# First cross-attention of an eight-layer kernel: output tiles copied by ScalarE and added to X by GpSimd, statistics one turn later

## The chip, the cores and the metric

One core of a Trainium2 chip. The metric is the device time of the whole program in microseconds (us).

## The reference, cut to what matters

The reference is a stack of four pairs of cross-attention and feed-forward network over `x` of shape (8, 256, 128), with a context of shape (8, 64, 128), all in fp32. Each member of a pair works on the normed stream and is added to it. The change touches the first attention and the statistics of the norm behind it:

```python
# first attention, on the layer-normed x; h = 16 heads of 8, one k head and one v head for all
q = x @ Wq
k, v = jnp.split(context @ Wkv, 2, axis=-1)
sim = jnp.einsum('bhnd,btd->bhnt', q * scale, k)
att = jax.nn.softmax(sim, axis=-1)
y = jnp.einsum('bhnt,btd->bhnd', att, v)
return y @ Wo            # added to the residual stream
# then the first feed-forward network (a soft mixture over 1024 slots) on the norm of that sum
```

## The kernel before, in words

The residual stream lives in SBUF as `X`, 16 tiles of 128 tokens by 128 features; batch b owns tiles 2b and 2b+1. The program is written per engine: each engine's order of work is written out by hand, and the engines are joined by semaphores. The first attention is a software pipeline over the 16 token tiles. Every engine has a loop over t (NT = 16), and one pass of it is called a turn here. In turn t:

- **TensorE**: `similarities(t)` (recorded as L1763) writes the 128x1024 scores of tile t into two PSUM banks; `weights_T(t-1)` transposes the exponentials of tile t-1 (eight transposes, L1820), once they are there; `values(t-2)` multiplies them with v and sums them (32 small matmuls, L1763); `outputs0(t-3)` multiplies tile t-3 with `wo0` into PSUM bank 7 (L1763). In turns 2, 6 and 10, called grouped turns, TensorE also transposes four tiles of the normed x and projects them to queries in the middle of the rest, and the transposes of the exponentials are split around that.
- **VectorE**: the maximum over the keys (L1343), the subtraction of the maximum (L1346), the reciprocal of the denominators of tile t-2 (L1354), the multiplication by it (L1355), and the addition of the output of tile t-3 to `X` out of PSUM (L1359), which signals `x_done`. In turn 5 it also takes the statistics of the slot embeddings (L1312 to L1318). After the fourth, eighth, twelfth and sixteenth addition, in turns 6, 10, 14 and 18, `norm_behind` takes the statistics of the four finished tiles for the next norm (L1229, L1232, L1236).
- **ScalarE**: in grouped turns the copies of the normed x and of the queries (L813, L843); then the copy of the transposed exponentials to SBUF (L813, 128x1024), then the exponential of tile t (L874, 128x1024).
- **GpSimd**: it builds the block-diagonal keys of batches 1 to 7 (`keys(b)`, L739), applies the norm to the slot embeddings (L753 to L755), and for each finished group of four tiles computes the power and applies the norm (`ln_power(1, g)`: L612, L619, L620).

`outputs0(u)` waits for `y_ready` (L1355 of tile u) and for `x_done` of tile u-1, since bank 7 holds one output. VectorE's maximum of turn t+1 stands in its queue behind everything of turn t. Behind the loop come the logits of the slots: `bmax(0)` (L1333) is VectorE's in turn 17; `bmax(1)`, `bmax(2)` and `brec(0)` follow its loop; GpSimd's L764 needs `brec(0)`, and TensorE's `dispatch_T(0)` (L1927) needs L764. ScalarE goes on with `bexp(0)` (L891).

Of the kernel before, what the change touches and what calls it, by code (L numbers as in the profile page):

```python
# [46 lines left out]
def build_program(nc, A, out):  # L47
    with ExitStack() as ctx:
# [111 lines left out]
        y0T = carve(2, P)  # L160
        mx0 = carve(2, H0)
        rden0 = carve(P)
        ctxTd = carve(B * 2 * C)
        slot_raw = carve(ES // P, D)
        slot_n = carve(ES // P, D)
# [167 lines left out]
        av_ready = sem("av_ready")  # L333
        y_ready = sem("y_ready")
        out_ready = sem("out_ready")
        bl_ready = sem("bl_ready")
        bmax_done = sem("bmax_done")
        bexp_done = sem("bexp_done")
# [236 lines left out]
        def _(pool):  # L575
# [151 lines left out]
            for L in range(LAYERS):  # L727
                if L == 7:
                    pool.wait_ge(x_done, NT * 6)
                    edges = xpad[:, :, :].rearrange("p h (b n) -> p h b n", b=B)  # L730
                    pool.memset(edges[:, :, :, 0:1].bitcast(F32), 0.0)
                    pool.memset(edges[:, :, :, N + 1:N + 2].bitcast(F32), 0.0)
                    pool.memset(share.bitcast(F32), 1.0 / 32.0).then_inc(pool_made, 1)
                    quantised_norm()
                    continue
                if L == 0:

                    def keys(b):
                        pool.tensor_tensor(kbd[:, b], wide(krep[:, b * C:(b + 1) * C].unsqueeze(1), H0 // 2, C),  # L739
                                           wide(rowmask[:, :].unsqueeze(2), H0 // 2, C), ALU.mult).then_inc(kbd_done[1], 1)  # L740

                    ln_power(0, 0)
                    ln_power(0, 1)
                    pool.wait_ge(krep_done, 1)
                    keys(1)
                    ln_power(0, 2)
                    keys(2)
                    keys(3)
                    ln_power(0, 3)
                    for b in range(4, B):  # L750
                        keys(b)
                    pool.wait_ge(se_var, 1)
                    then(pool.tensor_tensor(srstd[:, 1, :], srstd[:, 0, :], neghalf[:, 0:ES // P], ALU.pow))  # L753
                    then(pool.tensor_tensor(slot_n, slot_raw, wide(smv[:, :, 0:1], ES // P, D), ALU.subtract))
                    pool.tensor_tensor(slot_n, slot_n, wide(srstd[:, 1, :].unsqueeze(2), ES // P, D), ALU.mult).then_inc(se_n, 1)  # L755
                    continue
                for g in range(NG):
                    if L != 1 or g < NG - 1:
                        ln_power(L, g)
                if L == 1:  # L760

                    for k in range(4 * B):
                        pool.wait_ge(brec_done, k + 1)
                        pool.tensor_tensor(qb[:, k % 4], qb[:, k % 4], wide(recB[:, k % 4].unsqueeze(2), 2, N), ALU.mult)\  # L764
                            .then_inc(bnorm_done, 1)
                        if k == 3:
                            ln_power(1, NG - 1)
                    experts0_low()
                    pool.wait_ge(xh_lo, E0)
                    pool.memset(eo[:, :, :, D:D + 1], 1.0).then_inc(pool_made, 1)  # L770
                if L == 2:

                    pool.wait_ge(ln_xn, NG * L + NG)
                    pool.tensor_tensor(X[:, :, :], X[:, :, :], wide(rows[:, ROW["qv1_b"], :].unsqueeze(1), NT, D), ALU.add)\
                        .then_inc(xbias_done, 1)

                    then(pool.memset(sel1, 0.0))
                    per_expert = sel1.rearrange("p a (e i) -> p (a e) i", i=8)
                    then(pool.affine_select(out=per_expert, in_=per_expert, compare_op=ALU.not_equal, fill=1.0, base=0,
                                            pattern=[[-1, E1], [0, 8]], channel_multiplier=1))  # L780
                    pool.affine_select(out=per_expert, in_=per_expert, compare_op=ALU.not_equal, fill=1.0, base=-E1,
                                       pattern=[[-1, E1], [0, 8]], channel_multiplier=1).then_inc(pool_made, 1)
                if L == 3:
                    experts1_low()
                if L == 4:

                    pool.wait_ge(x_done, NT * L)
                    then(pool.memset(sel2, 0.0))
                    per_expert = sel2.rearrange("p g (e i) -> p (g e) i", i=P // 4)
                    for part in range(3):  # L790
                        last = pool.affine_select(out=per_expert, in_=per_expert, compare_op=ALU.not_equal, fill=1.0, base=-E2 * part,
                                                  pattern=[[-1, E2], [0, P // 4]], channel_multiplier=1)
                        if part < 2:
                            then(last)
                    last.then_inc(pool_made, 1)
                    pool.wait_ge(wgu_hi, STEPS0 + NC1 + 1)
                    pool.tensor_tensor(w2r[:, 1], w2all, w2r[:, 0].bitcast(F32), ALU.subtract).then_inc(wgu_lo, 1)
                if L == 5:
                    pool.wait_ge(x_done, NT * L)
                    experts2_low()  # L800
                if L == 6:
                    pool.wait_ge(ln_xn, NG * L + NG)
                    pool.tensor_tensor(X[:, :, :], X[:, :, :], wide(rows[:, ROW["o3_b"], :].unsqueeze(1), NT, D), ALU.add)\
                        .then_inc(xbias_done, 1)
                    for k in range(3):
                        pool.wait_ge(w3_hi, k + 1)
                        pool.tensor_tensor(hh[:, k, 1, :], w3f[:, k, :], hh[:, k, 0, :].bitcast(F32), ALU.subtract).then_inc(w3_lo, 1)
# [3 lines left out]
        def _(act):  # L811
# [39 lines left out]
            token_rows(0)  # L851
            queries(0)

            for t in range(NT + 3):
                g = (t + 2) // 4
                if t == 1:
                    act.wait_ge(kv_mm, 2)
                    act.wait_ge(consts, 2)
                    vps = psum[:, 6, 256:256 + B * HD].rearrange("p (b d) -> p b d", b=B)
                    for par in range(2):  # L860
                        for r in range(2):
                            at = 16 * par + HD * r
                            last = copy(vstrip[C * r:C * r + C, :, par, at:at + HD], vps[C * r:C * r + C])
                    last.then_inc(vstrip_done, 1)
                if t % 4 == 2 and t < NT - 2:
                    token_rows(g)
                    queries(g)
                if 1 <= t <= NT:
                    weight_rows(t - 1)
                if t < NT:  # L870
                    act.wait_ge(sim_used, t + 1)
                    if t >= 2:
                        act.wait_ge(et_ready, t - 1)
                    act.activation(simE[:, t % 2, :], simS[:, t % 2].rearrange("p h k -> p (h k)"), ACT.Exp).then_inc(exp_done, 1)  # L874
                if t == NT:

                    act.wait_ge(se_n, 2)
                    for g in range(2):
                        act.wait_ge(se_tp, g + 1)
                        act.activation(seT[:, 512 * g:512 * g + 512], bank(g), ACT.Identity, scale=slot_gs[:, 0:1], bias=slot_gs[:, 1:2])\  # L880
                            .then_inc(se_T, 1)
                    for g in range(2):
                        ln_evac_group(1, g)
# [329 lines left out]
        def _(dve):  # L1213
# [122 lines left out]
                        accum_out=nmB[:, k % 4, c:c + 1])  # L1336
                last.then_inc(bmax_done, 1)

            for t in range(NT + 3):
                if t < NT:  # L1340
                    dve.wait_ge(sim_ready, t + 1)
                    sim = psum[:, 2 * (t % 2):2 * (t % 2) + 2, :].rearrange("p a (h k) -> p (a h) k", k=C)
# [8 lines left out]
                if 2 <= t <= NT + 1:  # L1351
# [1 line left out]
                    dve.wait_ge(av_ready, u + 1)  # L1353
                    then(dve.reciprocal(rden0, psum[:, 6, P:2 * P]))  # L1354
                    dve.tensor_tensor(y0T[:, u % 2, :], psum[:, 6, 0:P], rden0, ALU.mult).then_inc(y_ready, 1)  # L1355
                if t >= 3:
                    u = t - 3
                    dve.wait_ge(out_ready, u + 1)
                    dve.tensor_tensor(X[:, u, :], X[:, u, :], psum[:, 7, 0:D], ALU.add).then_inc(x_done, 1)  # L1359
                    norm_behind(1, u)  # L1360
                if t == NT + 1:
                    bmax(0)

# [397 lines left out]
        def _(pe):  # L1761
# [75 lines left out]
            def outputs0(u):  # L1837
                if u == 0:
                    pe.wait_ge(w_slots, 16 * N_SLOTS)
                pe.wait_ge(y_ready, u + 1)  # L1840
                if u >= 1:
                    pe.wait_ge(x_done, u)
                mm(psum[:, 7, 0:D], y0T[:, u % 2, :], wo0[:, :]).then_inc(out_ready, 1)

            def logits_slots(k):
# [660 lines left out]
```

## Time and profile before

| | us |
|---|---|
| median of three runs (986.33 to 987.37) | 987.25 |
| the profiled execution, device time | 984.96 |
| its span | 983.2 |
| busy in the span: TensorE / VectorE / GpSimd / ScalarE | 913.7 / 719.9 / 572.7 / 521.5 |

The first attention takes the first tenth of the span: its first maximum starts at 12.66 us and its last addition at 90.65 us. The page's chain of waits reaches back only to 798 us, so this stage has to be read from its timeline. In a timeline row the bracket at the end gives the idle time of the engine just before it, and what ended it; gaps under 0.15 us are not shown. A row with xN stands for N instructions in one. Instructions of one engine overlap a little at their ends, so the distance between two starts can be shorter than the first one's duration.

### The profile page before, as it was taken

The page shows a single profiled execution, that of the slowest core. Times are in us where ns is not written, and L with a number is a line of the kernel's source. Part 1 is how long each engine was busy: PE and PEld are TensorE (multiplying, and loading weights), DVE is VectorE, ACT ScalarE, POOL GpSimd, SP SyncE. Part 2 cuts the span into 40 slices and gives each one's busy share as a digit, 9 for nine tenths or more (in the row PEclk, how much of TensorE's full clock was granted, in tenths as well). Part 3 has the DMA queues.
Part 4 walks back from the last instruction along what each step waited for, and adds up shares of the span by engine and source line. Part 5 has one row for each costly group of instructions (what it writes and reads, how often), then busy time and mean ns, then how long its engine had stood idle before and what let it go on. Part 6 is the DMA issues. An engine that isn't in the chain of part 4 may idle for free. (4 is left out here: it accounts for less than half of the span.)

```text
span 983.2 us, 16388 instructions
## 1 busy us (share of the span) xinstructions
PE 913.7 (93%) x4925; PEld 700.8 (71%) x4925; DVE 719.9 (73%) x1657; ACT 521.5 (53%) x991; POOL 572.7 (58%) x542
## 2 busy tenths in 40 slices
PE   7897998989896899999999999999999889999796
PEld 5555775666694856888888888888887766667564
DVE  6897776899464788766666666666667888886865
ACT  3455665544634256666666666666663334453354
POOL 5512544677513156777777777777776538884500
PEclk9999999999997989999999999999999689999998
DMA  6000000322000000000000000000002000000001
GB/s 193 1 2 2 1 1 11 88 71 66 12 1 27 2 9 14 25 25 24 24 24 24 24 24 24 24 24 24 25 3 108 1 0 1 1 1 1 1 11 33
DMA packets 27113, 24.01 MB, mean 24 GB/s; under 512 B 3420, under 2 KB 23988, under 8 KB 26804
## 3 DMA queue, kind: packets, MB, share of 16 engines
q1 hardware_dynamic: 27059, 23.34, 8.0%
q8 instruction: 29, 0.48, 0.2%
q14 instruction: 25, 0.20, 0.1%
HBM read 22.28 MB, written 1.05 MB: 24 GB/s over the span
## 5 line engine op out<-in xcount | busy, mean ns | idle before, releaser
L1763 PE MATMUL psum<-xw 128*128 128x512 f32 x1248 | 324.3, 396 | 3.9 <-DVE xw L1400 2.6
L664 POOL TENSOR_TENSOR hh<-arena,hh 128x512 fp32r<-128x512 f32 x176 | 228.2, 1296 | 81.7 <-ACT hh L813 80.0
L1763 PEld LDWEIGHTS psum<-xw 128*128 128x128 f32 x1248 | 233.4, 189 | 56.5 <-issue 7.2
L1599 DVE TENSOR_TENSOR psum<-psum,arena 128x512 f32<-128x512 f32 x176 | 123.1, 700 | 99.6 <-PE psum L1763 93.2
L813 ACT ACTIVATE hh<-arena 128x512 fp32r<-128x512 f32 x228 | 143.1, 629 | 47.7 <-DVE arena L1698 45.3
L1046 ACT ACTIVATE arena<-psum 128x512 f32<-128x512 f32 x176 | 105.3, 598 | 119.0 <-PE psum L1763 118.9
L1763 PE MATMUL psum<-hh,wdn 128*128 128x512 f32 x528 | 148.4, 390 | 0.2 <-POOL hh L664 0.2
L1604 DVE TENSOR_TENSOR arena<-psum,arena 128x512 f32<-128x512 f32 x176 | 121.7, 692 | 8.9 <-DVE psum L1599 2.9
L1763 PEld LDWEIGHTS psum<-hh,wdn 128*128 128x128 f32 x528 | 98.9, 188 | 21.1 <-POOL hh L664 0.5
L1763 PE MATMUL psum<-arena 128*32 128x128 f32 (+7 forms) x1032 | 94.0, 307 | 12.8 <-ACT arena L813 6.5
L612 POOL TENSOR_TENSOR rstd<-veps,neghalf 128x4 f32<-128x4 f32 x28 | 28.2, 1010 | 106.1 <-DVE veps L1238 76.0
L1763 PEld LDWEIGHTS psum<-arena 128*32 128x32 f32 (+4 forms) x1032 | 69.1, 148 | 25.0 <-issue 11.4
L813 ACT ACTIVATE arena<-psum 128x512 f32<-128x512 f32 (+7 forms) x84 | 57.1, 694 | 50.4 <-PE psum L1763 19.6
L701 POOL TENSOR_TENSOR hh<-arena,hh 128x512 fp32r<-128x512 f32 x48 | 62.1, 1295 | 33.3 <-ACT hh L813 31.8
L764 POOL TENSOR_TENSOR tail<-tail 128x512 f32<-128x512 f32 x32 | 33.3, 1041 | 43.4 <-DVE tail L1370 43.4
L1763 PE MATMUL psum<-hh,w2r 128*128 128x512 f32 x144 | 46.7, 417 | 2.0 <-POOL hh L701 1.0
L624 POOL TENSOR_TENSOR xw<-egu,xw 128x256 fp32r<-128x256 f32 x32 | 27.6, 864 | 31.8 <-ACT xw L813 31.5
L891 ACT ACTIVATE tail<-arena,tail 128x256 f32<-128x256 f32 x64 | 32.0, 500 | 26.1 <-DVE tail L1333 26.1
L928 ACT ACTIVATE tail<-psum,ebias 128x512 f32<-128x512 f32 x32 | 22.0, 688 | 44.5 <-PE psum L1763 36.9
L635 POOL TENSOR_TENSOR arena<-arena,xn (+1 forms) x32 | 42.8, 1343 | 1.2 <-ACT xn L813 1.2
L1690 DVE SCALAR_TENSOR_TENSOR arena<-psum,arena 128x512 f32<-128x512 f32 x48 | 33.1, 691 | 11.7 <-PE psum L1763 9.6
L1763 PE MATMUL psum<-xw,w2r 128*128 128x512 f32 x144 | 41.6, 401 | 0.0
(288 smaller groups left out, 1536.1 us busy)
## 6 DMA issues: line engine op xcount, KB each, us to landing
egu<-in_w SPq DMA_DIRECT2D x44, 128.0 KB, 2.0
egu<-in_egu SPq DMA_DIRECT2D x16, 256.0 KB, 2.6
edn<-in_w SPq DMA_DIRECT2D x44, 64.0 KB, 1.8
edn<-in_edn SPq DMA_DIRECT2D x16, 128.0 KB, 2.0
arena<-in_w SPq DMA_DIRECT2D x1, 1536.0 KB, 6.8
X<-in_x SPq DMA_DIRECT2D x4, 256.0 KB, 4.6
arena<-in_conv SPq DMA_DIRECT2D x1, 1024.0 KB, 8.8
out<-X SPq DMA_DIRECT2D x4, 256.0 KB, 2.3
```

The costliest lines, as they stand in the source:

```text
L612: pool.tensor_tensor(rstd[:, s], veps[:, s], neghalf[:, s], ALU.pow).then_inc(ln_rstd, 1)
L635: pool.tensor_tensor(part, part, wide(shift_row(b).unsqueeze(1), 2, N), ALU.subtract).then_inc(pt_shifted, 1)
L664: pool.tensor_tensor(hh[:, s % 4, 1, :], h1[:, s % 2, :], hh[:, s % 4, 0, :].bitcast(F32), ALU.subtract).then_inc(hh_lo, 1)
L701: pool.tensor_tensor(hh[:, n % 4, 1, :], h2[:, n % 2, :], hh[:, n % 4, 0, :].bitcast(F32), ALU.subtract).then_inc(hh_lo, 1)
L764: pool.tensor_tensor(qb[:, k % 4], qb[:, k % 4], wide(recB[:, k % 4].unsqueeze(2), 2, N), ALU.mult)\
L813: return act.activation(dst, src, ACT.Copy)
L891: last = act.activation(qb[:, k % 4, c, :], logit_part(k // 4, 2 * (k % 4) + c, 1).rearrange("p a n -> p (a n)"), ACT.Exp, scale=-1.0, bia ...
L1046: act.activation(sil[:, k, :], bank(k), ACT.Silu).then_inc(nl_done, 1)
L1599: dve.tensor_tensor(bank(2 + k), bank(2 + k), sil[:, k, :], ALU.mult).then_inc(prod_done, 1)
L1604: dve.tensor_tensor(h1[:, k, :], bank(2 + k), rwb[:, s // 4, own], ALU.mult).then_inc(hid_done, 1)
L1690: dve.scalar_tensor_tensor(v2w[:, n % 3, :], bank(q), 0.0, cB[:, 0 if n < 4 * NG else 1, 512 * q:512 * q + 512], ALU.max, ALU.mult)\
L1763: return pe.matmul(dst, lhsT=lhsT, rhs=rhs, start=start, stop=stop)
```

## The change

VectorE's addition in the loop is gone. ScalarE copies the output of tile t-4 from PSUM to one of two new SBUF buffers at the head of turn t, and GpSimd adds it to `X`. The loops of ScalarE and VectorE have one turn more. `outputs0(u)` waits for the copy and not for the addition. The statistics are taken in turns 7, 11, 15 and 19. GpSimd takes the additions between its other work, with `ln_power(1, 0)` to `ln_power(1, 2)` written out among them.

```diff
--- before.py
+++ after.py
@@ -160,6 +160,7 @@
         y0T = carve(2, P)
         mx0 = carve(2, H0)
         rden0 = carve(P)
+        o0 = carve(2, D)
         ctxTd = carve(B * 2 * C)
         slot_raw = carve(ES // P, D)
         slot_n = carve(ES // P, D)
@@ -333,6 +334,7 @@
         av_ready = sem("av_ready")
         y_ready = sem("y_ready")
         out_ready = sem("out_ready")
+        o0_sb = sem("o0_sb")
         bl_ready = sem("bl_ready")
         bmax_done = sem("bmax_done")
         bexp_done = sem("bexp_done")
@@ -747,15 +749,26 @@
                     keys(2)
                     keys(3)
                     ln_power(0, 3)
+
+                    def added(u):
+                        pool.wait_ge(o0_sb, u + 1)
+                        pool.tensor_tensor(X[:, u, :], X[:, u, :], o0[:, u % 2, :], ALU.add).then_inc(x_done, 1)
+
                     for b in range(4, B):
                         keys(b)
+                        added(b - 4)
                     pool.wait_ge(se_var, 1)
                     then(pool.tensor_tensor(srstd[:, 1, :], srstd[:, 0, :], neghalf[:, 0:ES // P], ALU.pow))
                     then(pool.tensor_tensor(slot_n, slot_raw, wide(smv[:, :, 0:1], ES // P, D), ALU.subtract))
                     pool.tensor_tensor(slot_n, slot_n, wide(srstd[:, 1, :].unsqueeze(2), ES // P, D), ALU.mult).then_inc(se_n, 1)
+                    added(4)
+                    for g in range(NG - 1):
+                        ln_power(1, g)
+                        for u in range(4 * g + 5, 4 * g + 9 if g < 2 else NT):
+                            added(u)
                     continue
                 for g in range(NG):
-                    if L != 1 or g < NG - 1:
+                    if L != 1:
                         ln_power(L, g)
                 if L == 1:
 
@@ -851,8 +864,14 @@
             token_rows(0)
             queries(0)
 
-            for t in range(NT + 3):
+            for t in range(NT + 4):
                 g = (t + 2) // 4
+                if t >= 4:
+                    u = t - 4
+                    act.wait_ge(out_ready, u + 1)
+                    if u >= 2:
+                        act.wait_ge(x_done, u - 1)
+                    copy(o0[:, u % 2, :], psum[:, 7, 0:D]).then_inc(o0_sb, 1)
                 if t == 1:
                     act.wait_ge(kv_mm, 2)
                     act.wait_ge(consts, 2)
@@ -1336,7 +1355,7 @@
                         accum_out=nmB[:, k % 4, c:c + 1])
                 last.then_inc(bmax_done, 1)
 
-            for t in range(NT + 3):
+            for t in range(NT + 4):
                 if t < NT:
                     dve.wait_ge(sim_ready, t + 1)
                     sim = psum[:, 2 * (t % 2):2 * (t % 2) + 2, :].rearrange("p a (h k) -> p (a h) k", k=C)
@@ -1353,11 +1372,8 @@
                     dve.wait_ge(av_ready, u + 1)
                     then(dve.reciprocal(rden0, psum[:, 6, P:2 * P]))
                     dve.tensor_tensor(y0T[:, u % 2, :], psum[:, 6, 0:P], rden0, ALU.mult).then_inc(y_ready, 1)
-                if t >= 3:
-                    u = t - 3
-                    dve.wait_ge(out_ready, u + 1)
-                    dve.tensor_tensor(X[:, u, :], X[:, u, :], psum[:, 7, 0:D], ALU.add).then_inc(x_done, 1)
-                    norm_behind(1, u)
+                if t >= 4:
+                    norm_behind(1, t - 4)
                 if t == NT + 1:
                     bmax(0)
 
@@ -1839,7 +1855,7 @@
                     pe.wait_ge(w_slots, 16 * N_SLOTS)
                 pe.wait_ge(y_ready, u + 1)
                 if u >= 1:
-                    pe.wait_ge(x_done, u)
+                    pe.wait_ge(o0_sb, u)
                 mm(psum[:, 7, 0:D], y0T[:, u % 2, :], wo0[:, :]).then_inc(out_ready, 1)
 
             def logits_slots(k):
```

## Rows read from the trace of the kernel before

**Rows 1.** Windows, turns 6 to 15: busy us of PE, PEld, DVE, ACT, POOL; PEclk.

```profile
43.00:86.00 43.00, 38.36 (x478) 25.16 (x477) 38.81 (x76) 22.93 (x25) 10.34 (x10) 0.98 0.01 2
```

**Rows 2.** Timeline of turns 7 and 8 (start us, duration us, instruction).

```profile
48.97 0.96 DVE L1354 RECIPROCAL arena<-psum 128x128 f32<-128x128 f32 x1 [0.64 <-PE psum L1763]
...
49.25 1.13 PE L1763 MATMUL psum<-arena 64*128 64x512 f32 x4
49.96 0.29 DVE L1355 TENSOR_TENSOR arena<-psum,arena 128x128 f32<-128x128 f32 x1
50.17 0.28 DVE L1359 TENSOR_TENSOR X<-X,psum 128x128 f32<-128x128 f32 x1
...
50.42 1.23 DVE L1343 TENSOR_REDUCE arena<-psum 128x16 f32<-128x1024 f32 x1
...
54.05 1.09 PE L1820 MATMUL psum<-ident,arena 128*128 128x128 f32 x8 [0.16 <-ACT arena L874]
```

**Rows 3.** Timeline of turns 11 and 12, TensorE and VectorE.

```profile
63.69 1.09 PE L1820 MATMUL psum<-ident,arena 128*128 128x128 f32 x8 [1.00 <-ACT arena L874]
...
65.86 0.96 DVE L1354 RECIPROCAL arena<-psum 128x128 f32<-128x128 f32 x1
...
67.32 1.23 DVE L1343 TENSOR_REDUCE arena<-psum 128x16 f32<-128x1024 f32 x1
```

**Rows 4.** Timeline of turns 14 and 15, VectorE, and GpSimd's norm of group 2.

```profile
74.88 1.22 DVE L1343 TENSOR_REDUCE arena<-psum 128x16 f32<-128x1024 f32 x1
...
78.78 0.87 DVE L1229 BATCH_NORM_STATS2 stats<-X 128x6 f32<-128x128 f32 x4
...
80.17 1.22 DVE L1343 TENSOR_REDUCE arena<-psum 128x16 f32<-128x1024 f32 x1
...
82.55 1.04 POOL L620 TENSOR_TENSOR xn<-xn,rstd 128x512 f32<-128x512 f32 x1
```

**Rows 5.** Groups by form (busy us, mean ns), nearest rows of the new operations.

```profile
L660 POOL TENSOR_TENSOR wdn<-edn,wdn 128x128 fp32r<-128x128 f32 x44 | 20.8, 473 | 0.0
...
L1124 ACT ACTIVATE arena<-psum 128x128 f32<-128x128 f32 x1 | 0.3, 278 | 2.2 <-PE psum L1763 2.2
```

**Rows 6.** Waits from 12 to 96 us: total us, times, longest us.

```profile
ACT arena L813 <- PE psum L1820: 18.6, 16, 1.5
```

**Rows 7.** Timeline of turn 10, TensorE's values and ScalarE's first copy.

```profile
58.15 1.08 PE L1763 MATMUL psum<-arena 128*32 128x128 f32 x32
58.26 0.60 ACT L813 ACTIVATE xnT<-psum 128x512 f32<-128x512 f32 x1 [0.48 <-PE psum L1800]
```

**Rows 8.** Timeline of GpSimd, the slot norm's first and last instruction.

```profile
38.47 1.64 POOL L753 TENSOR_TENSOR arena<-arena,neghalf 128x8 f32<-128x8 f32 x1 [7.82 <-DVE arena L1317]
...
42.17 1.90 POOL L755 TENSOR_TENSOR arena<-arena 128x1024 f32<-128x1024 f32 x1
```

**Rows 9.** Timeline of turn 6, TensorE's values.

```profile
39.85 1.08 PE L1763 MATMUL psum<-arena 128*32 128x128 f32 x32 [2.37 <-DVE arena L1355]
```

**Rows 10.** Timeline from turn 16 to the first dispatch transposes.

```profile
83.79 1.09 PE L1820 MATMUL psum<-ident,arena 128*128 128x128 f32 x8 [1.90 <-ACT arena L874]
...
89.52 0.29 DVE L1355 TENSOR_TENSOR arena<-psum,arena 128x128 f32<-128x128 f32 x1
...
90.15 0.46 PE L1763 MATMUL psum<-wo,arena 128*128 128x128 f32 x2 [0.40 <-DVE X L1359]
...
90.65 0.29 DVE L1359 TENSOR_TENSOR X<-X,psum 128x128 f32<-128x128 f32 x1
...
90.97 0.87 DVE L1229 BATCH_NORM_STATS2 stats<-X 128x6 f32<-128x128 f32 x4
...
95.08 0.66 PE L1927 MATMUL psum<-ident,tail 128*128 128x128 f32 x4 [2.30 <-POOL tail L764]
```

**Rows 11.** Windows as in Rows 1, two stretches for the clock.

```profile
42.00:45.00 3.00, 3.00 (x13) 2.24 (x13) 2.50 (x8) 0.83 (x2) 1.99 (x2) 0.56 0.00 0
80.00:84.00 4.00, 2.10 (x36) 1.67 (x26) 3.90 (x7) 1.71 (x2) 3.09 (x3) 1.00 0.01 2
```

## The prediction

> **What bounds the kernel now.** The chain of waits says nothing of this stage, so I read the windows for the load, then the timeline for what ends each wait. In the stretch of turns 6 to 15 VectorE is busy for 38.81 of 43 us and TensorE for 38.36 [rows 1]. Taken alone, that says that work off VectorE is time gained. The timeline says otherwise for most of it. What the reader is to see in turn 7: VectorE sits idle for 0.64 us and then takes the reciprocal at 48.97, because TensorE's values come late; after the multiplication (49.96) and the addition (50.17), the maximum of turn 8 starts at 50.42, just as TensorE's similarities end (49.25 + 1.13 = 50.38) [rows 2]. So even without the addition this maximum could not have started earlier. From it to the transposes in turn 8 (54.05) are 3.63 us, through VectorE's subtraction and ScalarE's exponential [rows 2]. From those transposes to the ones of turn 11 (63.69) are 9.64 us of the grouped turn 10, TensorE and ScalarE alone, and from there to the maximum of turn 12 (67.32) are again 3.63 [rows 3]. This ring of four turns takes 3.63 + 9.64 + 3.63 = 16.90 us, which is 67.32 - 50.42, and no addition stands in it. The statistics of turns 6 and 10 aren't in it either: they lie where VectorE waits for the grouped turn. Only turns 12 to 15 are VectorE's: the maxima of turns 12 and 14 are 7.56 us apart, 3.78 a turn [rows 3, 4], and in turn 14 the statistics, 1.39 us from their first instruction to the next maximum (78.78 to 80.17), stand on the path [rows 4].
>
> **The new work.** An unchanged row has the copy's very form, PSUM to SBUF, 128x128 on ScalarE, with 0.28 us. A 128x128 GpSimd operation on two whole tensors took 0.47 [rows 5]. Sixteen copies are 4.5 us and sixteen additions 7.5 us. The copies stand at the head of a turn, where ScalarE waits for the transposes: 18.6 us in sixteen waits, 1.16 each [rows 6]. In turn 10 the first copy has 0.48 us of idle time before it [rows 7], which the new one fits into. Without that cover each would cost its 0.28. The output that is copied was made a turn earlier, so it is there. Here the trace disagrees a little with a page of the Trainium skill (GPSIMD Engine Reference, Key points), which puts VectorE at about twice GpSimd's speed for elementwise work. By it an addition would be an estimated 0.56 us, twice the 0.28 of VectorE's [rows 2], and the sum below 0.09 higher.
>
> GpSimd's queue: the additions wait for ScalarE, and the keys, the slot norm and the powers are queued behind them. Keys 7 are not wanted before turn 14 and are made before the addition of tile 3. Behind that one the slot norm runs, 42.17 + 1.90 - 38.47 = 5.60 us [rows 8]. The addition of tile 3 can end at about 47.3 (exponential of turn 6 out at about 46.6, plus 0.28 and 0.47), so that of tile 4 at 47.3 + 5.6 + 0.5 = 53.4. ScalarE's copy of tile 6 waits for it, in turn 10, where its gap opens at 58.26 - 0.48 = 57.8 [rows 7]. That leaves 4.4 us: cost nothing. TensorE's output waits for a copy that is a turn older: nothing.
>
> **The sum**, on the times of the profiled execution. A step off VectorE's queue is 0.21 us, one start to the next (49.96 to 50.17) [rows 2].
>
> Turns 4 to 7. In turn 6 TensorE's values wait 2.37 us for VectorE's multiplication, which the slot statistics of turn 5 hold up [rows 9]. One addition ahead of it goes (the one before that ended a wait for TensorE anyway): -0.20, and all up to the reciprocal of turn 7 is that much earlier, 48.77.
>
> Turn 7. The statistics now stand between its multiplication (48.77 + 0.99 = 49.76) and the maximum of turn 8. They start at 49.97 and end in the maximum at 51.36 instead of 50.42: **+0.94**. This hangs on the 0.64 us wait ahead of the reciprocal: VectorE has no slack behind it. Their old place in turn 6 is left empty.
>
> Turn 11. Transposes of turn 8 at 51.36 + 3.63 = 54.99, of turn 11 at 64.63; the reciprocal 2.17 later (65.86 - 63.69 [rows 3]) at 66.80, multiplication 67.79, statistics 68.00, maximum of turn 12 at 69.39 instead of 67.32: **+2.07** in all.
>
> Turns 12 to 15. Here the additions and the statistics go off the path. A turn of VectorE becomes 3.78 - 0.21 = 3.57, but the ring through TensorE (3.63 down, 3.63 back) allows no less than 7.26 for two. Maximum of turn 14 at 69.39 + 7.26 = 76.65, of turn 15 at 76.65 + 3.57 = 80.22 instead of 80.17: **+0.05**. The statistics of turn 15 are hidden, since ahead of the transposes of turn 16 even TensorE waits 1.90 us [rows 10] and VectorE's next reciprocal comes later still.
>
> The end. The last output (90.15) waited for the addition before it; now it waits for the multiplication (89.52 + 0.05 + 0.29, and 0.12 as in the wait seen) and starts at 89.98, ends at 90.44 [rows 10]. Then come a copy (0.28), a GpSimd addition (0.47) and three hand-overs of about 0.05, as between 90.61 and 90.65: the last statistics start at about 91.35 instead of 90.97: **+0.4**, the 0.05 included. GpSimd is free by then: its power and norm of group 2 end 3.4 us after their statistics (83.59 after 80.17 [rows 4]). These now end near 80.22 + 3.36 + 0.2 + 1.39 = 85.2, so the norm ends at 88.6 and the additions of tiles 13 and 14 near 89.9. VectorE goes on from these statistics to `bmax(1)` and `brec(0)`, GpSimd's L764 and the transposes at 95.08, before which TensorE has waited 2.30 us [rows 10]. So it goes through whole.
>
> Sum +0.4: 984.96 becomes 985.4. The median shown is 2.3 above the profiled execution, so on its scale 987.25 becomes 987.6. Unknown: the GpSimd addition in the last link. At the least it is VectorE's 0.28, at the most the 1.64 that a small power of GpSimd took [rows 8], so +0.2 to +1.6; I take 0.47, the same shape and the same two inputs.
>
> **Rivals.**
> (a) Faster: VectorE bounds every turn. Then sixteen steps of 0.21 are 3.4 us, 983.9. For it speaks the load [rows 1]; against it the 0.64 wait and the maximum that starts as the similarities end [rows 2]. A half of it: the statistics of turns 7 and 11 cost nothing, as they do now in 6 and 10. Then the maximum of turn 12 comes at 67.12 and that of turn 15 at 77.95, 2.2 early, and with the end the time is 985.4. It needs at least 1.2 us of slack for VectorE between multiplication and maximum, where I see none. Together 0.15.
> (b) Slower: TensorE's clock falls in the holes that the statistics open. Ahead of the transposes of turn 8 TensorE waited 0.16 [rows 2]; these come 0.94 later and what stands before them 0.20 earlier, so it waits 1.30, and as long in turn 12. After a wait of 2.37 [rows 9] the granted clock was 0.56 of full speed, that is mostly its lower level of 1.2 GHz; through one of 1.90 it stayed at 1.00 [rows 10, 11]. The price: from the values of turn 6 to the next reciprocal 48.97 - 39.85 = 9.12 us, in turn 10 at full clock 65.86 - 58.15 = 7.71 [rows 2, 3, 7, 9], so 1.4 for each fall. One gives 989.1, two 990.5. It decides somewhere between waits of 1.90 and 2.37. The Trainium skill (TensorE: Matmul & The Clock Gate, Part 1) says that the gate follows how busy the engine has lately been and has just two states; the trace agrees. 0.12.
> (c) Slower: GpSimd's one queue. If the addition of tile 4 or 3 came 4.4 us later than I place it, ScalarE and the ring would stand behind the slot norm, up to its 5.6 us: 993. 0.05.
>
> **How the numbers follow.** My forecast has 0.68, and its own range is 987.3 to 988.9. A measurement can tell 0.2%, 2.0 us, from no change. The half of (a) and one fall of (b) stay within that. The range 985.4 to 989.5 takes both in and leaves out the whole of (a), two falls, and (c), some 0.17. Faster 0.13 is (a) nearly alone, slower 0.11 is (c) and the rest of (b), same 0.76.
>
> **What would show it.** Right: in turn 8 the maximum about 1.6 us behind the multiplication of turn 7 (now 0.46), and the same in turn 12; maxima of turns 12 to 15 some 3.6 apart; the idle time of VectorE grown in turns 6 and 10; the last statistics near 91.4, the first L1927 near 95.5. Wrong: a maximum of turn 8 at 50.2, a clock under 1.00 between 52 and 60, or GpSimd's L612 and the copies of ScalarE waiting long for one another in turns 8 to 10.

## The result, and the profile after

| | before | after |
|---|---|---|
| median of 13 runs each, us | 985.84 (983.11 to 987.37) | 988.78 (987.18 to 991.48) |
| ratio after/before, 95% interval | | 1.0034 (1.0025 to 1.0043) |
| profiled execution, us / its span | 984.96 / 983.2 | 987.18 / 985.5 |

The changed kernel is slower by 0.34%, 3.3 us, which is clear of noise. The time lies in the range I gave, 985.4 to 989.5, but the shift doesn't: I had +0.4 us and 0.76 for "within 0.2%", and only 0.11 for slower than that. That the time lies in the range is luck: the kernel before came out at 985.84 in these thirteen runs, 1.4 us under the 987.25 that the range was placed on. From 987.25 the same shift would have led to 990.6, outside it.

Line numbers have moved in the changed kernel: the maximum is L1362, the subtraction L1365, the reciprocal L1373, the multiplication L1374, the statistics L1248, L1251 and L1255, the exponential L893, the eight transposes L1836, the new copy L826 (128x128), the new addition L755, the slot norm L761 to L763. Times are compared as distances, since the whole stage starts 0.86 us sooner in this execution. "Transposes of turns 8 and 11" are, as in the prediction, those of the exponentials of tiles 8 and 10.

First the new operations, groups by form (busy us, mean ns, idle before):

```profile
L826 ACT ACTIVATE arena<-psum 128x128 f32<-128x128 f32 x16 | 4.3, 268 | 1.7 <-PE psum L1779 1.7
```

```profile
L755 POOL TENSOR_TENSOR X<-X,arena 128x128 f32<-128x128 f32 x16 | 7.3, 454 | 39.1 <-ACT arena L826 39.0
```

0.27 and 0.45 us, against 0.28 and 0.47 taken from [rows 5]. Their price isn't the matter. Turns 7 and 8 are, which answer to [rows 2] (timeline: start us, duration us, instruction):

```profile
45.20 1.23 DVE L1362 TENSOR_REDUCE arena<-psum 128x16 f32<-128x1024 f32 x1 [2.72 <-PE psum L1779]
...
48.32 0.96 DVE L1373 RECIPROCAL arena<-psum 128x128 f32<-128x128 f32 x1 [0.64 <-PE psum L1779]
...
49.31 0.29 DVE L1374 TENSOR_TENSOR arena<-psum,arena 128x128 f32<-128x128 f32 x1
49.52 0.86 DVE L1248 BATCH_NORM_STATS2 stats<-X 128x6 f32<-128x128 f32 x4
...
50.41 0.38 DVE L1251 BATCH_NORM_AGGREGATE mv<-stats 128x2 f32<-128x6 f32 x4
50.45 1.90 POOL L763 TENSOR_TENSOR arena<-arena 128x1024 f32<-128x1024 f32 x1
...
50.83 1.55 DVE L1255 TENSOR_SCALAR veps<-mv 128x4 f32<-128x4 f32 x1
...
52.29 1.21 DVE L1362 TENSOR_REDUCE arena<-psum 128x16 f32<-128x1024 f32 x1
...
55.90 1.89 PE L1836 MATMUL psum<-ident,arena 128*128 128x128 f32 x8 [2.67 <-ACT arena L893]
```

The wait ahead of the reciprocal is the same 0.64 us. Then three things are to be seen. The statistics start 0.21 behind the multiplication, as forecast. Their last instruction, four numbers per partition, takes 1.55 us instead of 0.17, and ends at 52.38, as GpSimd's L763 ends (50.45 + 1.90 = 52.35). And the transposes take 1.89 us instead of 1.09, behind a wait of 2.67. The windows (us, then busy us of PE, PEld, DVE, ACT, POOL; granted clock) say why the transposes were slow:

```profile
54.00:57.00 3.00, 1.10 (x6) 1.10 (x7) 2.97 (x4) 1.22 (x2) 2.35 (x3) 0.84 0.00 0
57.00:60.00 3.00, 3.00 (x40) 2.12 (x38) 1.61 (x3) 1.97 (x2) 0.00 (x0) 0.59 0.01 3
```

TensorE's granted clock was 1.00 up to 56 us and 0.50 to 0.52 in the three us behind, its lower level: it fell behind that hole. Turns 11 and 12 (as [rows 3]), 14 and 15 (as [rows 4]) and the end (as [rows 10]), again the timeline:

```profile
67.15 1.09 PE L1836 MATMUL psum<-ident,arena 128*128 128x128 f32 x8 [1.00 <-ACT arena L893]
...
71.91 1.22 DVE L1362 TENSOR_REDUCE arena<-psum 128x16 f32<-128x1024 f32 x1
...
82.75 1.21 DVE L1362 TENSOR_REDUCE arena<-psum 128x16 f32<-128x1024 f32 x1
...
93.08 0.28 ACT L826 ACTIVATE arena<-psum 128x128 f32<-128x128 f32 x1 [0.81 <-PE psum L1779]
...
93.44 0.45 POOL L755 TENSOR_TENSOR X<-X,arena 128x128 f32<-128x128 f32 x1 [0.63 <-ACT arena L826]
...
93.92 0.87 DVE L1248 BATCH_NORM_STATS2 stats<-X 128x6 f32<-128x128 f32 x4 [0.28 <-POOL X L755]
...
98.03 0.66 PE L1943 MATMUL psum<-ident,tail 128*128 128x128 f32 x4 [2.81 <-POOL tail L777]
```

Put together, from the first maximum to the first dispatch transposes (98.03 - 11.80 = 86.23 after, 95.08 - 12.66 = 82.42 before). The forecast column is the prediction's own numbers as differences:

| stretch | before | after | difference | forecast |
|---|---|---|---|---|
| first maximum to that of turn 7 | 33.18 | 33.40 | +0.22 | -0.20 |
| maximum of turn 7 to that of turn 8 | 4.58 | 7.09 | +2.51 | +1.14 |
| to the transposes of turn 8 | 3.63 | 3.61 | -0.02 | 0 |
| to those of turn 11 | 9.64 | 11.25 | +1.61 | 0 |
| to the maximum of turn 12 | 3.63 | 4.76 | +1.13 | +1.13 |
| to the maximum of turn 15 | 12.85 | 10.84 | -2.01 | -2.02 |
| to the last statistics | 10.80 | 11.17 | +0.37 | +0.33 |
| to the first dispatch transposes | 4.11 | 4.11 | 0 | 0 |
| sum | 82.42 | 86.23 | +3.81 | +0.4 |

So from turn 7 on the steps that I worked out stand to a few hundredths; two that I didn't have are missing, 1.37 us in turn 7 and 1.61 us behind turn 8. The first stretch went the other way than forecast.

The sum is longer than the difference of the two profiled executions, 2.2 us: this stage starts 0.86 us sooner after the change, and the stretch behind it is 0.8 us shorter (under stats_late below).

### The profile page after: what moved, and what is told of

It reads as the page before. It is cut to its first block and busy times, and to the rows that moved or that the text cites. A ratio compares the mean times of both kernels' runs of the same rounds, so it can differ in the third digit from the quotient of the medians.

```text
span 985.5 us, 16418 instructions
## 1 busy us (share of the span) xinstructions
PE 910.0 (92%) x4925; PEld 699.0 (71%) x4925; DVE 718.0 (73%) x1641; ACT 522.8 (53%) x1007; POOL 580.6 (59%) x558
## 5 line engine op out<-in xcount | busy, mean ns | idle before, releaser
L826 ACT ACTIVATE hh<-arena 128x512 fp32r<-128x512 f32 x228 | 142.5, 626 | 47.6 <-DVE arena L1714 45.4
L826 ACT ACTIVATE arena<-psum 128x512 f32<-128x512 f32 (+8 forms) x100 | 61.3, 625 | 50.5 <-PE psum L1779 20.3
```

The lines of the kernel that those rows point to most:

```text
L826: return act.activation(dst, src, ACT.Copy)
```

## The experiments

Each experiment is compared with the kernel before on the same chip, and has one trace of its own. A row shown is from the trace of the run it stands under, unless the text says otherwise. The theory: VectorE's L1255 waited for GpSimd's slot norm, which the additions had pushed later; the hole that this and the statistics made took the clock down.

**norm_early**: the slot norm out of the way.

```diff
 for b in range(4, B):
     keys(b)
-    added(b - 4)
+    if b < B - 1:
+        added(b - 4)
 ...
 (slot norm)
+added(3)
 added(4)
```

> The changed kernel with GpSimd's slot norm put back ahead of the addition of tile 3 (and so over by turn 7), nothing else. Lock theory: VectorE's small L1255 in turn 7 waited 1.38 us (1.55 instead of 0.17) because GpSimd was in the middle of the slot norm's last instruction. Here it takes 0.17, the maximum of turn 8 comes about 1.4 us earlier against the maximum of turn 7 (5.7 instead of 7.1), TensorE's wait before the transposes of that turn falls from 2.7 to about 1.3 us, the granted clock stays at 1.00 there, and the transposes of turns 8 and 11 are 9.6 apart instead of 11.3. Time 2.5 to 3 us under the changed kernel, about as before. Rival, the statistics alone open the hole: L1255 is 0.17 but the clock falls all the same, and the time is 1.4 us under the changed kernel, some 1.5 us above before. Rival, the long L1255 has another cause: it stays at 1.5 us.

987.62 us, ratio 1.0012 (1.0002 to 1.0022). Its timeline, turns 7 and 8:

```profile
51.55 0.17 DVE L1257 TENSOR_SCALAR veps<-mv 128x4 f32<-128x4 f32 x1
51.63 1.22 DVE L1364 TENSOR_REDUCE arena<-psum 128x16 f32<-128x1024 f32 x1
...
55.25 1.09 PE L1838 MATMUL psum<-ident,arena 128*128 128x128 f32 x8 [1.28 <-ACT arena L895]
```

The maximum of turn 8 comes 5.71 us after that of turn 7 (45.92), where I had 5.72. TensorE's wait is 1.28, the granted clock from 55 to 61 us is 1.00, and the transposes of turn 11 start at 64.89, 9.64 later. Against the changed kernel's 1.0034 that is 2.2 us back, a little under the 2.5 to 3 expected. Both rivals are out: the clock held, and the place of the slot norm is what made the long L1255. What is left over before can be placed in the trace. The stage is 0.78 us longer than before's (83.20 against 82.42), and the stretch behind it, to VectorE's first write of `xw`, 0.5 longer (70.96 against 70.48); together 1.3, where 1.2 was measured. The changed kernel was 0.8 shorter than before in that last stretch, so norm_early did not keep that gain.

**norm_late**, **norm_over_stats**, **norm_on_stats**: the wait by itself, made in the kernel before. The additions are VectorE's there, and only GpSimd's slot norm is held back, each time to another moment.

```diff
 pool.wait_ge(se_var, 1)
+pool.wait_ge(y_ready, 5)     # norm_late
+pool.wait_ge(q_sb, 3)        # norm_over_stats, in its place
+pool.wait_ge(q_mm, 3)        # norm_on_stats, in its place
```

> The kernel before, where only GpSimd's slot norm is held back by one more wait until the multiplication of turn 6 is done (y_ready 5), so that its second instruction lies over the statistics of turn 6. Lock theory: L1236 in turn 6 takes 1 to 1.6 us instead of 0.17 and ends when a GpSimd instruction ends; the maximum of turn 7 comes 1 to 1.4 us later, of which 0.6 gets through to the maximum of turn 8, so 0.5 to 1 us above before. The maxima and subtractions, which read PSUM, keep their 1.22. Rival, no lock: L1236 stays at 0.17 and the time is that of before within 0.3 us.

Missed: 987.16 us, ratio 1.0009 (0.9999 to 1.0018), and L1237 (the L1236 of before) kept its 0.17, under GpSimd's power, 1.40 us into it:

```profile
44.19 1.64 POOL L754 TENSOR_TENSOR arena<-arena,neghalf 128x8 f32<-128x8 f32 x1 [13.45 <-DVE arena L1356]
...
45.59 0.17 DVE L1237 TENSOR_SCALAR veps<-mv 128x4 f32<-128x4 f32 x1
```

> The kernel before, where only GpSimd's slot norm is held back until ScalarE has copied the queries of turn 6 (q_sb 3), so that its 128x1024 subtraction lies over L1236 of turn 6 (in the run norm_late L1236 met the power before it, of 128x8, and kept its 0.17). Lock theory: L1236 takes 1.2 to 1.5 us and ends as that subtraction ends; the maximum of turn 7 comes some 1.1 us later against that of turn 6. Time 0.3 to 1 us above before. Rival, VectorE's wait in the changed kernel came from something else of the change (the additions on X, which L1255's neighbours read): L1236 stays at 0.17.

Missed again by 0.12 us, at 986.71 us, ratio 1.0000 (0.9991 to 1.0009): L1237 began at 45.13 with 0.17, the subtraction only at 45.25.

> The kernel before, where GpSimd's slot norm is held back until TensorE has made the queries of turn 6 (q_mm 3), some 0.8 us sooner than in norm_over_stats, where the 128x1024 subtraction began 0.12 us after L1236 did. Now it starts about 0.6 us ahead of L1236 and covers it. Lock theory: L1236 takes 1.0 to 1.6 us instead of 0.17 and ends as the subtraction ends; the maximum of turn 7 waits for it; time 0 to 1 us above before. Rival, a cause other than GpSimd: L1236 keeps 0.17.

This time it met:

```profile
44.77 1.90 POOL L755 TENSOR_TENSOR arena<-arena 128x1024 f32<-128x1024 f32 x1
...
45.27 1.42 DVE L1237 TENSOR_SCALAR veps<-mv 128x4 f32<-128x4 f32 x1
...
46.61 1.21 DVE L1344 TENSOR_REDUCE arena<-psum 128x16 f32<-128x1024 f32 x1
```

1.42 us, over at 46.69, with the subtraction over at 46.67. The wait is shown without any other part of the change. It costs this kernel little, 986.17 us, 1.0005 (0.9996 to 1.0014). Part of it is taken up by the slack ahead of the reciprocal of turn 7: the maximum of turn 8 comes 3.77 us after that of turn 7, before 4.58. VectorE's maximum and subtraction, which read their scores from PSUM, keep 1.21 and 1.22 under GpSimd's next instruction of the same size (L756, 46.75 to 48.65), and the aggregation of the statistics (L1233, 44.86) keeps 0.38 under L755 itself.

The trace of the kernel before had this wait too, at the other end of the program, where the same small step of a later norm starts 0.08 us into a GpSimd instruction of 128x512:

```profile
908.40 1.04 POOL L722 TENSOR_TENSOR xn<-xn,rstd 128x512 f32<-128x512 f32 x1
908.48 0.98 DVE L1238 TENSOR_SCALAR veps<-mv 128x4 f32<-128x4 f32 x1
...
909.54 1.01 POOL L718 TENSOR_TENSOR rstd<-veps,neghalf 128x4 f32<-128x4 f32 x1
910.20 0.17 DVE L1291 TENSOR_SCALAR arena<-arena 128x4 f32<-128x4 f32 x1
```

0.98 us instead of 0.17, over at 909.46, with L722 over at 909.44. So the price could have been read before the change. The other pair is of use at the end: under GpSimd's power nothing waits.

**pe_filled**: the changed kernel with the hole filled, to price the clock.

```diff
 if 1 <= t <= NT:
     u = t - 1
+    if t in (9, 13):
+        pe.wait_ge(et_sb, u)
+        busy(4, 9 if t == 9 else 4)
     pe.wait_ge(exp_done, u + 1)
```

> The changed kernel with nine idle 128x128 matmuls ahead of TensorE's wait for the exponential in its turn 9 (the transposes of tile 8, where it stood still for 2.67 us) and four in its turn 13. Clock theory: of what the change lost, 1.6 us are TensorE's lower clock between 56 and 60 us. Here the granted clock stays at 1.00 there, the eight transposes take 1.09 instead of 1.89, the values 1.08 instead of 1.90, and the transposes of turns 8 and 11 are 9.6 us apart instead of 11.3; L1255 stays at about 1.5. Time 1.3 to 1.8 us under the changed kernel. Rival, the hole is not what lowers the clock, or the slow matmuls lay beside VectorE's work: no gain, or a loss of up to 0.5 us where the added matmuls outlast the wait.

988.00 us, ratio 1.0019 (1.0010 to 1.0028); by the ratios that is 1.5 us under the changed kernel. Timeline:

```profile
56.15 1.09 PE L1836 MATMUL psum<-ident,arena 128*128 128x128 f32 x8 [0.46 <-ACT arena L893]
...
65.79 1.09 PE L1836 MATMUL psum<-ident,arena 128*128 128x128 f32 x8 [1.00 <-ACT arena L893]
```

9.64 us again, L1255 still 1.55, the clock 1.00 from 55 to 61. So the 1.61 us are the clock's. The four matmuls in turn 13 shorten TensorE's wait there from 1.28 to 0.20 us and change no distance: the clock held there without them.

**after_again**: a second trace of the changed kernel.

> The changed kernel, unchanged, once more: a second trace of it. If the account is right, what the order of the work makes is there again: L1255 of turn 7 at about 1.55 us, the maximum of turn 8 some 7.1 us after that of turn 7, TensorE 2.67 us idle before the transposes of turn 8. The fall of the clock behind that hole may or may not come again; without it the transposes of turns 8 and 11 are 9.6 us apart, not 11.3. Ratio to before 1.0025 to 1.0045.

989.35 us, ratio 1.0036 (1.0024 to 1.0048). Both came again:

```profile
49.65 1.90 POOL L763 TENSOR_TENSOR arena<-arena 128x1024 f32<-128x1024 f32 x1
...
50.02 1.55 DVE L1255 TENSOR_SCALAR veps<-mv 128x4 f32<-128x4 f32 x1
...
51.49 1.21 DVE L1362 TENSOR_REDUCE arena<-psum 128x16 f32<-128x1024 f32 x1
...
55.10 1.97 PE L1836 MATMUL psum<-ident,arena 128*128 128x128 f32 x8 [2.67 <-ACT arena L893]
```

The transposes of turns 8 and 11 are 11.20 apart (54.28 - 43.08 from the first maximum on). The whole stage is 85.17 here, not 86.23: the other stretches from turn 7 on agree within 0.1 us, and the first one is 32.37 where it was 33.40.

**before_again**: the kernel before against itself.

> The kernel before, unchanged, against itself: what the comparison and one profile can tell. Ratio 1.000 within 0.001. In the profile the distances between maxima up to turn 15 as in the first one within 0.1 us, except where the granted clock of TensorE fell at another place; if those places move from one execution to the next, single profiles can't be compared to better than the 0.7 to 1.6 us that one fall costs.

985.35 us, ratio 0.9996 (0.9987 to 1.0005). The distances from the first maximum to the others agree to 0.12 us up to turn 15, and to the first dispatch transposes it is 82.41 (82.42). With after_again, the rows of the table from turn 7 on are not noise of single traces. Its first row is less certain: the two traces of the changed kernel differ by 1.03 us there.

**stats_late** and, unchanged, **stats_late_2**: only the place of the statistics, in the kernel before.

```diff
-for t in range(NT + 3):
+for t in range(NT + 4):
 ...
-if t >= 3:
+if 3 <= t < NT + 3:
     (addition of tile t - 3)
-    norm_behind(1, u)
+if t >= 4:
+    norm_behind(1, t - 4)
```

> The kernel before with only the statistics one turn later (turns 7, 11, 15, 19); the additions stay with VectorE, GpSimd's order is the old one. Theory: statistics that stand between the multiplication and the next maximum delay the ring. Maximum of turn 8 later by 1.3 us against the maximum of turn 7 (5.9 instead of 4.6), the same again in turn 12, L1236 at 0.17 because the slot norm is over, then 1.4 won back in turn 14; TensorE's wait ahead of the transposes of turn 8 about 1.5, clock 1.00. Time 1 to 1.5 us above before. Rival, the statistics are free where they are put: the maxima stay where they are and the time falls by 1.4 us. Rival, the clock falls in these holes too: 2.5 to 4 us above before.

985.13 us, ratio 0.9988 (0.9978 to 0.9997): faster, where I expected slower. The trace has the stretches as expected (5.91 us between the maxima of turns 7 and 8, L1236 at 0.17, the clock at 1.00 behind this wait), and the first dispatch transposes 1.36 us later:

```profile
51.28 0.17 DVE L1236 TENSOR_SCALAR veps<-mv 128x4 f32<-128x4 f32 x1
51.36 1.22 DVE L1343 TENSOR_REDUCE arena<-psum 128x16 f32<-128x1024 f32 x1
...
54.98 1.09 PE L1821 MATMUL psum<-ident,arena 128*128 128x128 f32 x8 [1.48 <-ACT arena L874]
```

> The same kernel as stats_late (before, statistics one turn later), since its time (0.12% under before, interval 0.03 to 0.22%) and its trace (first dispatch transposes 1.4 us later than before) disagree. If the ring arithmetic holds for the whole time, the ratio is 1.001 to 1.002 this time. If the executions with other places of the lower clock make up for it, it is again at 0.998 to 0.9995 and the trace shows the same 1.4 us.

985.84 us, 0.9998 (0.9989 to 1.0008), dispatch transposes 1.13 us later. Neither run came out at the 1.001 to 1.002 that the stage says. A part is visible in the traces, in the windows behind the first dispatch transposes. First the kernel before, then the changed one:

```profile
95.00:98.00 3.00, 2.92 (x13) 2.52 (x14) 1.45 (x6) 0.25 (x2) 1.02 (x2) 0.64 0.02 5
```

```profile
98.00:101.00 3.00, 2.83 (x16) 2.22 (x16) 2.10 (x8) 0.80 (x5) 1.45 (x2) 1.00 0.02 5
```

The clock falls there in both traces of before and stays up in these two and in both of the changed kernel. From there to VectorE's first write of `xw` it takes 70.5 us in the traces of before and 69.7 in the four others. That is 0.8 us back. The rest of the difference stays open.

**group2_late**: of the statistics, only those of tiles 8 to 11 moved; nothing else of the change.

```diff
-    norm_behind(1, u)
+    if u != 11:
+        norm_behind(1, u)
+    if u == 12:
+        norm_behind(1, 11)
```

> The kernel before with the statistics of tiles 8 to 11 alone moved from turn 14 to turn 15; additions, the other statistics and GpSimd's order are the old ones. Theory: in turn 14 they stand on the path (VectorE bounds turns 12 to 15), in turn 15 they lie in the wait for TensorE. Maximum of turn 15 against that of turn 12: 11.3 instead of 12.9 us, the first dispatch transposes about 1.4 us earlier. Time 1.0 to 1.5 us under before. Rival, another wait takes their place: no change.

982.47 us (six runs), ratio 0.9967 (0.9954 to 0.9979). Timeline, from the maximum of turn 12 to the moved statistics (L1229) and the dispatch:

```profile
65.47 1.23 DVE L1343 TENSOR_REDUCE arena<-psum 128x16 f32<-128x1024 f32 x1
...
76.81 1.22 DVE L1343 TENSOR_REDUCE arena<-psum 128x16 f32<-128x1024 f32 x1
...
80.43 1.09 PE L1823 MATMUL psum<-ident,arena 128*128 128x128 f32 x8 [0.38 <-ACT arena L874]
80.59 0.86 DVE L1229 BATCH_NORM_STATS2 stats<-X 128x6 f32<-128x128 f32 x4
...
91.73 0.67 PE L1930 MATMUL psum<-ident,tail 128*128 128x128 f32 x4 [2.30 <-POOL tail L764]
```

11.34 us between the two maxima instead of 12.85, and as long as before (14.92, before 14.91) from the second to the dispatch: 1.5 us that come through whole. The measured 3.3 us (2.1 to 4.5) are more than that. In its trace TensorE also kept the full clock in turn 6, and the maximum of turn 8 comes 1.4 us sooner after the first one than before; whether it does so in most executions isn't known. This one change of order beats both kernels.

**stats_placed**: norm_early with the statistics where VectorE waits, and `ln_power` moved behind the additions they need.

```diff
-if t >= 4:
-    norm_behind(1, t - 4)
+if t in (10, 14, 15, NT + 3):
+    norm_behind(1, {10: 3, 14: 7, 15: 11, NT + 3: 15}[t])
```

> The kernel norm_early (changed kernel, slot norm early) with the statistics put where VectorE waits: tiles 0 to 3 in turn 10, 4 to 7 in turn 14, 8 to 11 in turn 15. Theory: copies and additions off VectorE cost the ring nothing, only the place of the statistics did. The maximum of turn 8 comes 4.4 us after that of turn 7 (5.7 in norm_early), the transposes of turns 8 and 11 stay 9.6 apart, and the first dispatch transposes come 1.2 to 1.5 us earlier than in norm_early against the first maximum. Time 1 to 1.5 us under norm_early, within 0.7 us of before. Rival, the copies and additions themselves hold up the ring: no gain over norm_early.

986.95 us, 1.0008 (0.9999 to 1.0017), 0.4 to 0.7 us under norm_early instead of 1 to 1.5. Timeline, maxima of turns 7 and 8, then turns 14 and 15:

```profile
46.04 1.23 DVE L1366 TENSOR_REDUCE arena<-psum 128x16 f32<-128x1024 f32 x1 [2.75 <-PE psum L1783]
...
50.62 1.23 DVE L1366 TENSOR_REDUCE arena<-psum 128x16 f32<-128x1024 f32 x1 [0.17 <-PE psum L1783]
...
74.78 1.23 DVE L1366 TENSOR_REDUCE arena<-psum 128x16 f32<-128x1024 f32 x1
...
78.37 0.86 DVE L1252 BATCH_NORM_STATS2 stats<-X 128x6 f32<-128x128 f32 x4
...
79.75 1.22 DVE L1366 TENSOR_REDUCE arena<-psum 128x16 f32<-128x1024 f32 x1
```

4.58 us, exactly that of before (I had 4.4), with no addition and no statistics on VectorE, which now even waits for TensorE. This settles the faster rival: VectorE's additions were worth nothing in this turn.

The dispatch transposes are at 82.47, before's 82.42. But this order isn't the best one, which is why the gain missed: the statistics of tiles 4 to 7, put into turn 14, stand on VectorE's path there. The maximum of turn 15 comes 4.97 us after that of turn 14, in norm_early 3.59. Without these 1.4 us the stage would be near 81.1, an estimate. The kernel before with its one group moved (group2_late) would be at 80.9 with before's turn 6 (79.51 + 1.4), also an estimate. So with the statistics well placed in both, sixteen additions taken off VectorE leave the stage about as long. The traces show what cancels: with its statistics in the same turns, stats_late takes 11.34 us from the maximum of turn 12 to that of turn 15, the changed kernel 10.84; and the changed kernel's end is 0.37 longer than before's.

**last_on_dve**: stats_placed with tile 15 added by VectorE; ScalarE's copy and GpSimd's addition of that tile are gone (not shown here).

```diff
+if t == NT + 3:
+    u = NT - 1
+    dve.wait_ge(out_ready, u + 1)
+    dve.tensor_tensor(X[:, u, :], X[:, u, :], psum[:, 7, 0:D], ALU.add).then_inc(x_done, 1)
```

> The kernel stats_placed with the last tile alone (15) added by VectorE out of PSUM as before. Theory: the copy and the GpSimd addition before the last statistics cost 0.7 to 0.8 us; the last statistics come 0.7 us earlier against the first maximum than in stats_placed, and the dispatch transposes too. Time 0.4 to 0.8 us under stats_placed, near before or 0.5 under it. Rival: hidden behind TensorE's logits, no change.

985.29 us, ratio 0.9991 (0.9980 to 1.0003). But the trace doesn't bear out the reason: from the last multiplication to the last statistics it takes 1.79 us (77.14 - 75.35 from the first maximum on), in stats_placed 1.84 (78.36 - 76.52). `bmax(0)` stands between them and hides nearly all of the copy and the GpSimd addition. The 1.2 us that its dispatch transposes come earlier were nearly all gained before turn 7, 0.9 of them in turns 0 to 3: from 12 to 22 us the granted clock was 1.00 there, in stats_placed 0.83. Another 1.3 us lie behind the dispatch transposes (69.66 to `xw`, 70.96 in stats_placed), where the clock kept its full speed. So the median 1.7 us under stats_placed, more than expected, is no proof of the theory. The rival is right that the step is hidden.

## Why the prediction failed

- **The ring and its arithmetic, from turn 7 on: right.** The maximum of turn 8 is 5.71 us behind that of turn 7 in norm_early (forecast 5.72), turn 11 costs 1.13 (1.13), turns 12 to 15 give back 2.01 (2.02). TensorE, not VectorE, ends the waits of turn 8; stats_placed shows it.
- **The cost of copies and additions: right**, 0.27 and 0.45 us, hidden. GpSimd's queue as such too: ScalarE's copy of tile 6 waited 0.28 us, and for TensorE.
- **The step that failed is in the paragraph on GpSimd's queue, which ends in "cost nothing".** I asked only who waits in GpSimd's queue. I had the slot norm moved over turns 7 and 8 and ending near 52.9, and the statistics ending at 51.4, and did not ask whether the two engines get in each other's way. They do: 1.37 us in turn 7, shown by norm_early and norm_on_stats. The hole grew by that to 2.67 us, the clock fell behind it, and this cost another 1.61 us, shown by pe_filled. The Trainium skill (SBUF — State Buffer, Who interferes with whom) says that VectorE and GpSimd share a pair of ports as an exclusive lock, held for the whole instruction, and that a VectorE `tensor_scalar` in SBUF can need it. The traces agree for this step, with 1.55 and 1.42 us; they differ from it under GpSimd's power (last section). That page was there for me to weigh against the change, and so was the row of 0.98 us in the trace of before.
- **Turns 4 to 7, -0.20: swallowed**, by what looks like the same lock. The additions also push `keys(7)` (L741) over the slot statistics of turn 5, here in the trace of the changed kernel:

```profile
36.51 1.04 POOL L741 TENSOR_TENSOR arena<-arena,rowmask 128x512 f32<-128x512 f32 x1
...
37.03 0.55 DVE L1336 TENSOR_SCALAR arena<-arena 128x8 f32<-128x8 f32 x1
```

  0.55 us where it was 0.17, over as L741 is. From the maximum of turn 4 to that of turn 6 it is 10.11 us, before 10.12: the 0.20 won and these 0.38 about cancel. No run tests this one alone. What is left in turn 6 (0.2 to 0.4 us) stays open. In turns 0 to 3 the two traces of the changed kernel differ by 0.9 us (clock 0.83 in one and 1.00 in the other from 12 to 22 us).
- **Rival (b), the clock: right in mechanism and nearly in price** (1.4 a fall, measured 1.61 and 1.56), but not for the wait that it was given. I set it at 0.12 for a wait of 1.30 us. The sign that I had named for being wrong, a clock under 1.00 between 52 and 60, is there, with 0.79. With the statistics alone the clock did hold, through 1.28 in norm_early and 1.48 in stats_late. With the lock on top the wait was 2.67, and the clock fell in both traces. The two missing terms have one root: without the lock the wait is 1.28, and the clock holds.
- **Rival (a), faster: out**, by the 4.58 us of stats_placed. Its half, statistics that cost nothing in turns 7 and 11, is out by the 1.13 us of turn 11.
- **A small slip in the numbers:** by its own "+0.2 to +1.6" the forecast's range starts at 987.45, not at 987.3.

## What to carry to other kernels

Work that is moved to GpSimd also moves what stands behind it in GpSimd's queue. Lay every long GpSimd instruction, at its new time, over VectorE's small `tensor_scalar` steps on SBUF; a step of 0.17 us can cost as much as what is left of the GpSimd instruction. Search the trace that you have for such a step that is already long somewhere. And ask of each group of statistics whether it stands in a turn where its engine waits anyway: moving one group by one turn was worth 1.5 us of this stage, and sixteen additions taken off VectorE left it about as long.

## What I had not expected of the hardware

GpSimd's power didn't block VectorE's small steps, though its multiplications and subtractions did. In norm_late L1237 ran in 0.17 us, 1.40 us into a power of 1.64 on 128x8. In the trace of before, L1291 ran in 0.17, 0.66 us into a power of 1.01 on 128x4 (rows shown above). The operations of 128x1024 stretched L1255 and L1237, one of 128x512 L1238, and one of 128x512 goes with the long L1336.

The length of a wait alone doesn't decide on TensorE's clock either, so the prediction's "somewhere between waits of 1.90 and 2.37" doesn't hold at either end. The wait of 1.90 us before the transposes of turn 16 left the clock at 1.00 in both traces of the kernel before (82 to 88 us). It stands the same 1.90 in norm_late, norm_over_stats and norm_on_stats, with the clock at 0.72 from 82 to 88 us in all three. And in group2_late a wait of 2.36 us before the values of turn 6 was followed by 1.00 from 40 to 46 us. Transposes of norm_late:

```profile
82.95 1.73 PE L1821 MATMUL psum<-ident,arena 128*128 128x128 f32 x8 [1.90 <-ACT arena L875]
```
